# The GCN neighbour sum of a two-layer graph kernel: a separate gather and scatter pass replaced by slot tables in DRAM and one-hot products inside the next stage

## The reference, cut to what matters

```python
h = relu(layernorm(x))
h = relu(batchnorm(h @ w1.T + b1)); h = h @ w2.T + b2; xw = h @ w_gcn.T
norm = dinv[src] * dinv[dst]                 # dinv = 1/sqrt(degree)
out = segment_sum(xw[src] * norm[:, None], dst, n) + b_gcn
x = x + out                                  # first layer
h = relu(layernorm(x))
q, k, v = (h @ Wq + bq) * scaling, h @ Wk + bk, h @ Wv + bv   # 8 heads
e = exp(s - segment_max(s, src)); s = (q[src] * k[dst]).sum()  per head
x = x + segment_sum(e / z * v[dst], src) @ Wo + bo
```

## Time and profile before

| what | us |
|---|---|
| time of three runs, median (lowest to highest) | 4466.4 (4462.04 to 4470.41) |
| time of the profiled execution | 4477.67 |
| its span, first to last instruction | 4475.9 |
| mean granted TensorE clock | 0.953 |
| stage B, first to last | 747.7 to 1267 |
| GCN pass, with its barrier | 1271 to 2121.6 |
| stage C | 2121.6 to 3250 |
| stage E | 3282 to 4476 |

### The profile page before, as it was taken

One profiled execution on the slowest core, in us unless ns is written; L12 is line 12 of the kernel. 1 busy time (PEld: TensorE's weight loads), 2 busy tenths in 40 slices (PEclk: granted clock), 3 DMA queues, 4 the chain that ended last, 5 costly groups with the idle time before them and its releaser, 6 DMA issues. The chain is left out here.

```text
span 4475.9 us, 90147 instructions
## 1 busy us (share of the span) xinstructions
PE 3651.3 (82%) x23250; PEld 2846.7 (64%) x23250; DVE 3570.8 (80%) x10146; ACT 2576.2 (58%) x7493; POOL 2242.1 (50%) x1593
## 2 busy tenths in 40 slices
PE   4999996678856666665788888888849999999999
PEld 2555554566634444443677777777738999989998
DVE  7999996962277888787788888888858888888887
ACT  3666664567722222222555555555538888888887
POOL 1000001345557777776666666666535555555553
PEclk8999998899989999998899999999969999999999
DMA  2444443679944444444899999999846666666663
GB/s 89 155 159 155 155 159 135 249 296 350 353 115 77 76 76 77 75 76 74 302 323 329 327 327 326 329 322 327 298 168 225 235 221 233 228 226 232 226 231 135
DMA packets 293631, 947.79 MB, mean 212 GB/s; under 512 B 51514, under 2 KB 84666, under 8 KB 280967
## 3 DMA queue, kind: packets, MB, share of 16 engines
q1 hardware_dynamic: 173350, 677.00, 43.0%
q0 software_dynamic: 106048, 218.26, 17.6%
q10 hardware_dynamic: 14112, 51.39, 2.8%
HBM read 500.36 MB, written 497.59 MB: 223 GB/s over the span
## 5 line engine op out<-in xcount | busy, mean ns | idle before, releaser
L1873 ACT ACTIVATE e_acc<-e_acc,e_attention 128x32 f32<-128x32 f32 x3136 | 685.6, 310 | 33.0 <-DVE e_attention L2010 22.8
L1466 PE MATMUL c_qkv_ps<-w_qkv_hi,c_ht_hi 128*128 128x256 f16 x2352 | 662.0, 281 | 0.0
L1466 PE MATMUL c_qkv_ps<-w_qkv_lo,c_ht_hi 128*128 128x256 f16 x2352 | 661.6, 281 | 0.0
L1466 PE MATMUL c_qkv_ps<-w_qkv_hi,c_ht_lo 128*128 128x256 f16 x2352 | 660.3, 281 | 0.0
L831 PE MATMUL mix_ps<-w_mix,hb 128*128 128x256 f32 x1568 | 384.1, 401 | 131.2 <-ACT hb L805 72.4
L1828 POOL DMA_INDIRECT e_kv<-kv_table,e_near x392 | 427.4, 1090 | 124.5 <-issue 99.8
L1006 POOL DMA_INDIRECT agg_table<-gcn_summed,gcn_goal x240 | 388.5, 1619 | 138.9 <-DVE gcn_keys L969 55.2
L831 PEld LDWEIGHTS mix_ps<-w_mix,hb 128*128 128x128 f32 x1568 | 305.6, 200 | 210.2 <-ACT hb L805 99.2
L1280 ACT ACTIVATE gcn_summed<-gcn_sum_ps 128x256 f32<-128x256 f32 x240 | 92.2, 384 | 588.1 <-PE gcn_sum_ps L1263 457.5
L1392 POOL TENSOR_TENSOR c_qk<-c_q,c_kv 128x1024 f32<-128x1024 f32 x98 | 231.4, 2361 | 383.9 <-DVE c_kv L1494 383.9
L1820 POOL TENSOR_TENSOR e_kv<-e_kv,e_part_of 128x1024 f32<-128x1024 f32 x98 | 188.4, 1922 | 438.2 <-DVE e_part_of L2033 438.2
(11 more groups left out here) (333 smaller groups left out, 10351.1 us busy)
## 6 DMA issues: line engine op xcount, KB each, us to landing
kv_table<-c_kv SPq DMA_DIRECT2D x98, 1024.0 KB, 7.8
acc_table<-c_acc SPq DMA_DIRECT2D x98, 544.0 KB, 3.0
e_acc<-acc_table SPq DMA_DIRECT2D x98, 544.0 KB
h_table<-h POOLq DMA_DIRECT2D x98, 512.0 KB, 2.9
h<-h_table SPq DMA_DIRECT2D x98, 512.0 KB, 5.2
y_table<-y_out ACTq DMA_DIRECT2D x98, 512.0 KB, 4.9
agg_table<-agg_out POOLq DMA_DIRECT2D x98, 512.0 KB, 5.3
c_agg<-agg_table SPq DMA_DIRECT2D x98, 512.0 KB, 5.0
```

The lines of the kernel that those rows point to most:

```text
L1466: last = nc.tensor.matmul(qkv_ps[n][:, j * D:(j + 1) * D], h[u][:, kc, j * P:(j + 1) * P], w[:, kc, n * D:(n + 1) * D], start=m == 0, stop ...
L1873: last = nc.scalar.activation(mine, mine, ACT.Copy, scale=attention[u][:, j, h, 0:1])
```

## The change

The pass over 240 columns is gone, and with it the packing by parity. In its place:

1. Stage B begins with 14 rounds on DVE, two groups of 8 edges in each (L984 to L991), which list each partition's edges in `found`, and then a chain (L1003 to L1052) which works out for every edge a goal (a slot, lane times 392 plus subtile) by target and a word. Since the edges are sorted by target, a partition's edges belong to at most eight subtile classes, and the chain counts within classes.
2. Beside the mixing, POOL puts the words into DRAM: for each group of 8 columns two small copies and 8 indirect DMAs of 128 words of 4 bytes into `dst_slots`, and 8 more into `src_slots`, whose goals the sort by source gives, which now runs beside the mixing (16 columns in each body of 6 tiles, 13 bodies). The node's own share moves from POOL to ACT, its store from POOL to SP.
3. After the mixing both tables are loaded and unpacked. A new one-column loop takes what does not fit; here nothing.
4. Stage C gathers y rows for each tile (4 indirect DMAs, the slots of the 4 subtiles), DVE makes 4 one-hot matrices, PE multiplies, DVE adds the sum to agg. All later steps of a tile move back by three. The three products share two PSUM buffers, and DVE's order is changed.

The core of it, shortened:

```diff
+                    with dve.Fori(0, takes) as i:          # before the first tile of stage B
+                        for h in halves:
+                            v.max(out=best[:, :], in_=words[:, :]).then_inc(best_ready, 1)
+                            hold(dve, best_ready, i * 2 + (h + 1))
+                            v.tensor_copy(found[:, bass.ds(i * TAKEN + h * SLOTS, SLOTS)], best[:, :].bitcast(I32))
+                            v.match_replace(out=words[:, :], in_to_replace=best[:, :], in_values=words[:, :],
...
+                    pe.wait_ge(class_ready, 1)
+                    for q in classes:
+                        last = nc.tensor.matmul(total[:, 0:subtiles], class_low[:, q, :], class_hot[:, q, :], start=q == 0, stop=q == CLASSES - 1)
...
+                            for j in range(ROWS):
+                                last = nc.scalar.activation(agg_out[u][:, j, :], mix[u][:, j, :], ACT.Copy,
+                                                            scale=own_scale[:, bass.ds(tile * ROWS + j, 1)])
...
+                    def put_by_dst(i, h):
+                        hold_past(pool, dst_put[h], i * 16 * SLOTS)
+                        at = bass.ds(i * TAKEN + h * SLOTS, SLOTS)
+                        pool.tensor_copy(staged_goal[h][:, :], dst_goal[:, at])
+                        pool.tensor_copy(staged_word[h][:, :], dst_word[:, at]).then_inc(dst_staged, 1)
+                        hold(pool, dst_staged, i * 2 + (h + 1))
+                        for k in range(SLOTS):
+                            put(dst_slots, staged_goal[h], staged_word[h], k).then_inc(dst_put[h], 16)
+                    def put_by_src(i, h):
+                        hold(pool, src_goals_ready, i * 2 + (h + 1))
+                        for k in range(SLOTS):
+                            put(src_slots, src_goal[h], src_word[h], k).then_inc(src_put[h], 16)
...
-            @block.gpsimd                                   # the GCN pass
-                        gather(got[k][:, :], y_table, c["ends"][k][:, 0:1]).then_inc(gathered[k], 16)
-                        scatter(agg_table, c["goal"][k][:, 0:1], summed[k][:, :], compute_op=ALU.add).then_inc(c["scattered"][k], 16)
...
-            qkv_ps = [part.enter_context(nc.psum_tensor(f"c_qkv_ps{i}", [P, ROWS * D], F32)) for i in range(3)]
+            qkv_ps = [part.enter_context(nc.psum_tensor(f"c_qkv_ps{i}", [P, ROWS * D], F32)) for i in range(2)]
+            sum_ps = part.enter_context(nc.psum_tensor("c_sum_ps", [P, ROWS * D], F32))
...
+                    if at(1) is not None:                   # POOL in stage C, between qk and bias
+                        hold(pool, near_ready, tile_of(at(1)) + 1)
+                        for j in range(ROWS):
+                            nc.gpsimd.indirect_dma_start(out=got[w][:, j, :], out_offset=None, in_=y_table,
+                                                         in_offset=bass.IndirectOffsetOnAxis(ap=near[w][:, j:j + 1], axis=0),
+                                                         bounds_check=TAB - 1, oob_is_err=False).then_inc(got_landed[w], 16)
...
+                        for j in range(ROWS):               # PE, tile 3 behind
+                            last = nc.tensor.matmul(sum_ps[:, j * D:(j + 1) * D], sum_hot[w][:, j, :], got[w][:, j, :], start=True, stop=True)
...
+                        v.tensor_tensor(agg[w][:, :, :], sum_ps[:, :].rearrange("p (j d) -> p j d", j=ROWS), agg[w][:, :, :],
+                                        ALU.add).then_inc(summed, 1)
...
+                        for j in range(ROWS):               # DVE, last in the step, tile 2 behind
+                            last = v.tensor_scalar(sum_hot[w][:, j, :], lane[:, 0:P], sum_lane[:, bass.ds(tile * ROWS + j, 1)], None, ALU.is_equal)
```

1123 lines of the change are left out of this document (618 added, 505 removed).

## The result

The changed kernel takes **4904.4 us** (median of 4 runs, 4902.2 to 4907.8) against 4464.2 us (4459.6 to 4470.4) for the kernel before: a ratio of 1.0986, 95% interval 1.0967 to 1.1005. The prediction said 4745 us with a range up to 4870. The direction was right, the size was not, and the time lies above the range.

The account below looks back on a forecast made before the run. Before: POOL bounds the GCN pass, transfers bound stage B, and in C all engines are partly idle. 4477.7 - 9 (preparation) - 443 (pass and B) + 731 (C) = 4757 profiled, 11 above the median: 4745 us, range 4350 to 4870.

Parts of the forecast that it names:

- Head of B: Start of stage B: bn chain 10, 28 rounds 68, chain about 30 us; 108 us that nothing covers.
- Bodies of B: Stage B's 13 bodies of 6 tiles with 32 puts: POOL bounds them, 44.4 us each, 577 us in all.
- rival of dear puts: Stage B: as the main case, but puts up to 1.9 us or held by DVE; 4800 to 4945 us, chance 0.10.
- The bounds for dearer puts: Stage B's total if puts cost more: 960 us at 1.5 us a put, 1140 at the scatter-add's price.
- Behind the mixing: End of stage B: 56 puts left, 78 us with copies and waits, then 9 to load and unpack the tables.
- the loop: One-column loop after B, run once: an estimated 16 us, plus two barriers, 9.
- main case: Whole kernel: POOL-bound bodies in B, 19.0 us a tile in C; 4745 us, own range 4640 to 4850, chance 0.58.
- The B term: Stage B with the one-column loop: 931 us against 1374 before for B, pass and barrier, -443 us.
- Stage C: Masked scores and copy wait for POOL's adds, POOL for the second evacuation: 19.0 us a tile, 1860 against 1129, +731.
- The slip-through at 14.7: Stage C rival: DVE reaches the masked scores before the bias add, 14.7 us a tile; 4366 us, chance 0.21.
- the rival of that name: Alternating turns in stage C: some blocked, some not, 16 to 17 us; 4500 to 4560 us, chance 0.07.
- The price of a put beside busy DVE: Stage B's puts: the undisturbed 1.31 us taken, though the skill's 3100 ns would make 464 puts about 830 us dearer.

Follow-up runs that it names:

- hot_last: Changed kernel with stage C's gathers ahead of POOL's x1 add and DVE's turn reordered, one-hot rows last: 4250.8 us, 0.9541 of the kernel before.
- few_puts: Changed kernel with only 1 of every 8 puts issued, on chip 2: mixing took 600 us, no PE signal surely late.

## Why the prediction was wrong, step by step

- **Head of B** (108 us): 742.1 to 833.3 is 91 us. The order and the exposure were right, PE waited 110.06 us ahead of its first class product. The 28 rounds took 62.6 us (68), and the chain lasts 31 us as forecast, but only its first 16 stand ahead of PE's class product; the rest runs beside PE's first mixing products.
- **Bodies of B** (44.4 us each, 577): **the step that failed.** "So POOL bounds the bodies" held on chips 2, 11 and 14 (42.9 us a body on 14), but where the result was measured a body took 61.5 us and POOL waited. The rival of dear puts has the measured time in its range (4800 to 4945), but that is chance: the puts weren't dear (0.98 us). That PE's signals arrive up to 13 us late and SyncE's steps take 0.7 us beside a train of puts was in no case of the prediction, and no row of before shows it. Why they do is open. The bounds for dearer puts were also added up too low: over 464 puts the sum of 906 gives 994 us at 1.5 us a put (960 written) and 1175 at 1.89 (1140 written).
- **Behind the mixing** (78 + 9) and the loop (25): 1723.6 to 1811.9 is 88 us, then 28 to the first load of C; 116 against 112.
- On chip 14 the same sum reads: B and loop 742.2 to 1607.1, 865 us (predicted 931); C 1825 (1860); span 4645.5 against 4757 predicted. There the measured 4643 lies inside the main case's own range of 4640 to 4850, at its edge. The B term was 66 us too dear (head 17, mixing 31, most of the rest the filling of the pipeline).
- **Stage C** (19.0 us a tile): right in mechanism in the main and within 5% in size, 18.1 (18.8 inside the stage). The blocked copy and POOL's wait for the second evacuation are in the rows above, the blocked masked scores in 19 of 32 turns; in the 13 others the bias add holds the row scales. The slip-through at 14.7 didn't come about; it took hot_last's two orders to get near it. The turns alternate, but not at the 16 to 17 us of the rival of that name. PE was misjudged: it is busy 405 of 600 us, where the prediction had under half, and DVE waits 5.21 us for PE's sum in the turn shown, so PE's chain lies inside the period, which the prediction left out ("nothing waits for PE there").
- **The price of a put beside busy DVE**: the Trainium skill (SBUF — State Buffer, "A bandwidth-pool intuition that's wrong") gives about 3100 ns for a GpSimd DMA under a DVE copy; measured are 981 ns over 102 puts in 400 us, with DVE busy 172.6 of them, mostly on other instructions than copies. The measurement decides for this mix. The Trainium skill's rule on small transfers (DMA: Bandwidth & Descriptors, "Specifications": under 512 B they are read-modify-writes) shows no difference between writes and reads here: reads of the same words made mixing some 7 us longer, not shorter, on chips that don't stall.
- The range was built from terms of one chip's trace. Nothing in it stood for the chip, though chip to chip the changed kernel spreads by 350 us (4643 to 4993), the kernel before by 29.

## What to carry to other kernels

Some short DVE operations on SBUF last as long as the POOL product they meet, so in a loop where both engines take turns the order in which they meet can decide more than their busy times. Put those beside POOL's gathers, and what reads PSUM beside POOL's products (18.1 to 14.0 us a tile here, with no work taken away). Here it held for a product or SCALAR_TENSOR_TENSOR of SBUF operands, COPY and TENSOR_SCALAR. It didn't hold for row statistics, which took their usual 0.4 us beside POOL's bias add at 2509.12 of the earlier trace rows, nor for TENSOR_REDUCE: of 53 in stage C of the kernel before, the 20 that started inside a POOL product took 1.19 us like the rest. When a kernel issues long trains of indirect transfers of single words, time it on more than one chip before sizing or blaming anything, and compare edits only on the same chip. Before counting signals in a trace, see how many of them it holds. An experiment without its control on the same chip can seem to prove a cause: few_puts did.
